# Post-norm attention and ternary FFN on one core: two raw quarters of the second FFN matrix wait in the first norm's columns and in x rows, their sums move behind the first matrix's rounds, and signs take the place of clips

## The reference

```python
x = _layernorm(x + _L0_attn_ref(x, Wq, Wk, Wv, betas, Wo))
x = _layernorm(x + _L0_ffn_ref(x, W1, b1, W2, b2))

def _quantize(W):
    gamma = jnp.mean(jnp.abs(W))
    return jnp.clip(jnp.round(W / (gamma + EPS)), -1.0, 1.0)
# in _L0_ffn_ref: d = 512, d_ff = 2048
Wq1, Wq2 = _quantize(W1), _quantize(W2)
h = jax.nn.relu(jnp.einsum('bsd,fd->bsf', x, Wq1) + b1)
out = jnp.einsum('bsf,df->bsd', h, Wq2) + b2
```

## Time and profile before

| | us |
| --- | --- |
| median of 3 runs (1894.05 to 1895.91) | 1894.54 |
| the profiled execution, its own time | 1894.47 |
| its span | 1892.5 |
| TensorE busy | 1848.2 |
| VectorE busy | 1450.5 |
| ScalarE busy | 1001.9 |
| mean granted TensorE clock | 0.994 |

### The profile page before, as it was taken

How to read it: one execution, slowest core, us unless ns; L and a number is a source line. 1 busy time by engine, 2 the same in 40 slices (tenths; PEclk the granted TensorE clock), 3 DMA queues, 4 the chain that set the end, 5 groups by cost and what they waited for, 6 DMA issues and landing times.

```text
span 1892.5 us, 44351 instructions
## 1 busy us (share of the span) xinstructions
PE 1848.2 (98%) x16447; PEld 1306.4 (69%) x16447; DVE 1450.5 (77%) x2935; ACT 1001.9 (53%) x2422; POOL 765.2 (40%) x775
## 2 busy tenths in 40 slices
PE   5789999999999999999999999999999999999998
PEld 3666677776667776667776677776677776677765
DVE  7868777778777778777777777778777778777774
ACT  5765555555555555555555555555555555555541
POOL 1214334444334444334444334444334444344442
PEclk9899999999999999999999999999999999999999
DMA  8422333422333323323322333323333323233110
GB/s 272 125 44 33 62 58 62 68 48 52 63 59 60 68 44 55 64 55 64 68 47 51 64 59 60 68 48 52 60 62 60 68 47 52 59 59 63 36 24 23
DMA packets 556420, 117.47 MB, mean 62 GB/s; under 512 B 529824, under 2 KB 533808, under 8 KB 555696
## 3 DMA queue, kind: packets, MB, share of 16 engines
q1 hardware_dynamic: 556208, 114.64, 30.9%
HBM read 50.54 MB, written 16.80 MB: 36 GB/s over the span
## 4 chain that ended last, share of the span: by engine, by line
PE 93%; DVE 4%; ACT 1%; SPq 1%; issue 1%; DMA 0%; another core or an unknown queue 0%; POOLq 0%; DVEq 0%; POOL 0%; ACTq 0%
PE bank L433 12%; PE bank L434 12%; PE bank L449 11%; PE bank L450 11%; PE bank L282 6%; PE bank L283 6%; PE bank L284 6%; PE bank L370 3%; PE bank L415 3%; PE bank L414 3%; PE bank L413 3%; PE bank L296 3%; PE bank L349 3%; PE bank L298 3%; PE bank L297 3%; PE bank L401 2%
## 5 line engine op out<-in xcount | busy, mean ns | idle before, releaser
L433 PE MATMUL bank<-yt,w1t 128*128 128x256 f16 x2048 | 453.9, 273 | 0.3 <-DVE yt L811 0.2
L434 PE MATMUL bank<-yt,w1t 128*128 128x256 f16 x2048 | 453.9, 273 | 0.0
L1154 ACT ACTIVATE prob<-bank,exp_bias,gscalars 128x128 f32<-128x128 f32 x512 | 227.7, 456 | 360.4 <-DVE exp_bias L728 356.2
L449 PE MATMUL bank<-w2t,arena 128*128 128x512 f16 x1024 | 388.4, 379 | 0.0
L450 PE MATMUL bank<-w2t,arena 128*128 128x512 f16 x1024 | 388.1, 379 | 0.0
L1198 ACT ACTIVATE arena<-bank,b_scaled,wscalars 128x256 f32<-128x256 f32 x512 | 263.0, 570 | 205.3 <-PE bank L434 151.8
L863 DVE CAST arena<-arena 128x512 f16<-128x512 f32 x256 | 154.3, 603 | 92.8 <-ACT arena L1198 92.0
L1323 POOL TENSOR_TENSOR att_mem<-att_mem,gate_in 128x512 f32<-128x512 f32 x60 | 86.6, 1444 | 330.5 <-DVE att_mem L767 320.2
L433 PEld LDWEIGHTS bank<-yt,w1t 128*128 128x128 f16 x2048 | 200.5, 98 | 23.8 <-issue 0.6
L434 PEld LDWEIGHTS bank<-yt,w1t 128*128 128x128 f16 x2048 | 200.3, 98 | 22.7
L1401 POOL TENSOR_TENSOR arena<-arena 128x512 f16<-128x512 f32 x128 | 155.2, 1213 | 86.1 <-DVE arena L863 86.1
(11 more groups left out here) (186 smaller groups left out, 4299.9 us busy)
## 6 DMA issues: line engine op xcount, KB each, us to landing
rows<-in_L_attn_x SPq DMA_DIRECT2D x32, 512.0 KB, 3.8
out_rows<-rows SPq DMA_DIRECT2D x64, 256.0 KB, 2.3
x_blocks<-in_L_attn_x SPq DMA_DIRECT2D x248, 64.0 KB, 3.0
sk<-sk_t SPq DMA_DIRECT2D x480, 32.0 KB, 2.0
att_dot<-att_mem SPq DMA_DIRECT2D x480, 32.0 KB, 2.0
y_blocks<-rows SPq DMA_DIRECT2D x480, 32.0 KB
arena<-in_L_ffn_W SPq DMA_DIRECT2D x6, 1024.0 KB, 5.3
w2t<-in_L_ffn_W SPq DMA_DIRECT2D x2, 1024.0 KB, 13.1
```

The costliest lines, as they stand in the source:

```text
L433: pe.matmul(ps[:, c], w1t[:, k, cols], yt[:, g % 2, :, k], start=k == 0, stop=False)
L434: ins = pe.matmul(ps[:, c], w1t[:, k, cols], yt[:, g % 2, :, KT + k], start=False, stop=k == KT - 1)
L449: pe.matmul(banks[own][:], h_hi[:, f, toks], w2t[:, f, :], start=f == 0, stop=False)
L1154: ins = act.activation(prob[:, t, at], ps[:, c], ACT.Exp, scale=gcol(g, G_EXP), bias=exp_bias[:, t, at:at + 1], accum_out=row_sum[:, t, h: ...
```

## The change

**Places.** (2,1) now waits in `yt`, the columns of the first norm (both of its halves), (2,3) in rows 1 and 2 of the x buffer; both get semaphores of their own and are loaded early, with no wait for a free arena slot. (2,2) still takes the arena slot of (1,2). Only one copy for a sum remains, that of (2,2); it is loaded behind (1,3) into w1t and is summed by ScalarE where (2,1) was.

**Sums.** VectorE sums (2,1) and (2,3) in their places, behind `round_w(3)`; its two earlier sums are gone. The loads of a turn on SyncE are reordered, and x rows 1 and 2 are loaded at the end of turn g = 1, row 1 behind a wait for all 32 turns.

**Way out.** `put_w` takes Sign(x - ROUND), which is -1, 0 or 1 already. The eight `clip_w` and both waits for them go; `ffn_up` and `ffn_down` wait for `wput` alone.

The diff, without the lists of semaphores:

```diff
@@ -162,7 +162,7 @@
         MOVED = 16 * 16
-        SUM_ORDER = [(1, 1), (1, 3), (1, 0), (1, 2), (2, 0), (2, 1)]
+        SUM_ORDER = [(1, 1), (1, 3), (1, 0), (1, 2), (2, 0), (2, 2)]
         EDGES = (0, NG - 1)
@@ -203,17 +203,21 @@
         def ffn_raw(m, i):
             if m == 1 and i < 2:
                 return w2t[:, 8 * i:8 * i + 8].rearrange("p f n -> p (f n)").bitcast(F32)
+            if (m, i) == (2, 1):
+                return yt[:].rearrange("p g t k n -> p (g t k n)").bitcast(F32)
+            if (m, i) == (2, 3):
+                return rows[:, 1:3].rearrange("p g t d -> p (g t d)")
             return arena[:, (i + 2) % 4, :]
         def ffn_raw_loaded(m, i):
-            if m == 1 and i < 2:
-                return s_raw[4 + i], 16
+            if m == 1 and i < 2 or m == 2 and i % 2:
+                return s_raw[4 + i if m == 1 else 5 + (i + 1) // 2], 16
             slot = (i + 2) % 4
-            return s_raw[slot], {(1, 2): 32, (1, 3): 32, (2, 0): 32, (2, 1): 32, (2, 2): 48, (2, 3): 48}[m, i]
-
-        def for_sum(i):
-            return w1t[:, :, (i - 2) * F // 2:(i - 1) * F // 2].bitcast(F32)
+            return s_raw[slot], {(1, 2): 32, (1, 3): 32, (2, 0): 32, (2, 2): 48}[m, i]
+
+        def for_sum():
+            return w1t[:, :, 0:F // 2].bitcast(F32)
         def w_bank(n):
@@ -424,7 +428,6 @@
                 if n >= 2:
                     pe.wait_ge(sem["relu"], n - 1)
                 else:
-                    pe.wait_ge(sem["clipped"], 4)
                     pe.wait_ge(sem["wput"], NBLOCKS - 3 + n)
                 pe.wait_ge(sem["yt"], by_t(g, 1))
                 for c in range(2):
@@ -442,7 +445,7 @@
                 if piece == 0 and g:
                     pe.wait_ge(sem["res1"], by_t(g - 1, t))
                 elif piece == 0:
-                    pe.wait_ge(sem["clipped"], 8)
+                    pe.wait_ge(sem["wput"], NBLOCKS)
                 pe.wait_ge(sem["h_dve"], 4 * g + piece + 1)
                 pe.wait_ge(sem["h_pool"], 4 * g + piece + 1)
                 for f in range(piece * FT // PIECES, (piece + 1) * FT // PIECES):
@@ -895,9 +898,9 @@
                 dve.scalar_tensor_tensor(out=w_lo[n][:, :, cols], in0=raw[n][:, :, cols], scalar=w(SCALE_W[n]),
                                          in1=w_hi[n][:, :, cols], op0=ALU.mult, op1=ALU.subtract).then_inc(sem["wsplit"], 1)
-            def w_sum(i):
-                dve.wait_ge(s_raw[4 + i], 16)
-                dve.tensor_reduce(w(SUM_PART[2] + i), for_sum(i), AX_XY, ALU.add,
+            def w_sum(m, i):
+                dve.wait_ge(*ffn_raw_loaded(m, i))
+                dve.tensor_reduce(w(SUM_PART[m] + i), ffn_raw(m, i), AX_X, ALU.add,
                                   apply_absolute_value=True).then_inc(sem["wsum_dve"], 1)
             def threshold(m):
@@ -916,12 +919,6 @@
                 dve.wait_ge(*ffn_raw_loaded(m, i))
                 raw_w = ffn_raw(m, i)
                 dve.tensor_scalar(raw_w, raw_w, w(INV_STEP[m]), ROUND, ALU.mult, ALU.add).then_inc(sem["rounded"], 1)
-
-            def clip_w(n):
-                m, i = 1 + n // 4, n % 4
-                dve.wait_ge(sem["wput"], 4 * n + 4)
-                part = w1t[:, :, i * 512:(i + 1) * 512] if m == 1 else w2t[:, :, i * P:(i + 1) * P]
-                dve.tensor_scalar(part, part, 2.0, -1.0, ALU.min, ALU.add).then_inc(sem["clipped"], 1)
             def ffn_scale():
                 dve.wait_ge(sem["bias_turn"], 1)
@@ -986,8 +983,6 @@
                 h_split(g - 2, 5)
                 turn_att(g - 1, 0)
                 qk_split(g, "k", 1)
-                if g == 1:
-                    clip_w(4)
                 if g == 0:
                     w_max("o")
                 turn_att(g - 1, 1)
@@ -999,10 +994,6 @@
                     w_split("v", 0)
                     w_chain("o")
                 qk_split(g, "q", 1)
-                if g == 2:
-                    clip_w(5)
-                    clip_w(6)
-                    clip_w(7)
                 if g == 0:
                     w_split("v", 1)
                 residual(g - 1, 0, 0)
@@ -1020,12 +1011,9 @@
                 turn_x(g + 1, 0)
                 turn_x(g + 1, 1)
                 if g == 0:
-                    w_sum(2)
                     ffn_scale()
                 turn_sk(g)
                 v_split(g, 0)
-                if g == 0:
-                    w_sum(3)
                 invert_sums(g, 0)
                 if g == 0:
                     threshold(1)
@@ -1048,6 +1036,8 @@
                 turn_y(g - 1, 1)
                 if g == 0:
                     round_w(3)
+                    w_sum(2, 1)
+                    w_sum(2, 3)
                 p_split(g, 1, 0)
                 all_max(g + 1)
                 x_scale(g + 1, 0)
@@ -1065,19 +1055,12 @@
                     round_w(4)
                 att_scale(g, 0)
                 read_scale(g, 1)
-                if g == 0:
-                    clip_w(0)
                 xt_lo(g + 1, 0)
                 att_scale(g, 1)
-                if g == 0:
-                    clip_w(1)
                 xt_lo(g + 1, 1)
                 normalise(g - 2, 0, 1)
                 residual(g - 2, 1, 1)
                 h_split(g - 1, 0)
-                if g == 0:
-                    clip_w(2)
-                    clip_w(3)
                 mem_add(g, 0)
                 if g == 0:
                     round_w(5)
@@ -1206,7 +1189,11 @@
             def w_sum(m, i):
                 dst, src = unread, ffn_raw(m, i)
-                act.wait_ge(*ffn_raw_loaded(m, i))
+                if (m, i) == (2, 2):
+                    dst, src = unread.rearrange("p (k f) -> p k f", k=KT), for_sum()
+                    act.wait_ge(s_raw[8], 16)
+                else:
+                    act.wait_ge(*ffn_raw_loaded(m, i))
                 if SUM_ORDER.index((m, i)):
                     act.wait_ge(sem["wsum"], SUM_ORDER.index((m, i)))
                 act.activation(dst, src, ACT.Abs, accum_out=w(SUM_PART[m] + i)).then_inc(sem["wsum"], 1)
@@ -1217,10 +1204,10 @@
                 ps = banks[w_bank(n)][:].rearrange("p (j c) -> p j c", j=4)
                 dst = w1t[:, :, f0:f0 + P] if m == 1 else w2t[:, b * 4:b * 4 + 4, i * P:(i + 1) * P]
                 if n == 0:
-                    act.wait_ge(sem["wsum_dve"], 2)
+                    act.wait_ge(sem["wsum"], 6)
                     act.wait_ge(sem["ones"], 1)
                 act.wait_ge(sem["wturn"], n + 1)
-                act.activation(dst, ps, ACT.Relu, bias=unround[:]).then_inc(sem["wput"], 1)
+                act.activation(dst, ps, ACT.Sign, bias=unround[:]).then_inc(sem["wput"], 1)
             def gates():
                 act.wait_ge(sem["bload"], 16)
@@ -1274,7 +1261,7 @@
                 exponentials(g, 1, 1)
                 p_split(g, 0, 1)
                 if g == 0:
-                    w_sum(2, 1)
+                    w_sum(2, 2)
                     for n in range(0, 4):
                         put_w(n)
                 p_split(g, 1, 0)
@@ -1406,7 +1393,7 @@
                                channel_multiplier=1).then_inc(sem["ident"], 1)
             pool.memset(minus_half[:], -0.5).then_inc(sem["half"], 1)
             pool.memset(ones_all[:], 1.0)
-            pool.memset(unround[:], 1.0 - ROUND)
+            pool.memset(unround[:], -ROUND)
             pool.memset(v1[:, :, :, DV:DV1], 1.0).then_inc(sem["ones"], 1)
             for live in range(LIVE):
                 fill_memory(0, live)
@@ -1447,6 +1434,8 @@
                 if g >= NX:
                     for t in range(TG):
                         sp.wait_ge(s_out[g % NX][t], 16 * (g // NX))
+                if g == 1:
+                    sp.wait_ge(sem["wturn"], NBLOCKS)
                 if g == NX - 1:
                     sp.wait_ge(sem["wsum"], 6)
                 sp.dma_start(rows[:, g % NX], src).then_inc(s_x[g % NX], 16)
@@ -1467,20 +1456,17 @@
             def load_w(n):
                 sp.dma_start(raw[n], dram_w[n].rearrange("(k p) n -> p k n", p=P)).then_inc(s_raw[W_AT[n]], 16)
-            def load_for_sum(i):
-                src = W2.rearrange("(i p) (k f) -> i p k f", p=P, k=KT)[i]
-                sp.dma_start(for_sum(i), src).then_inc(s_raw[4 + i], 16)
+            def load_for_sum():
+                src = W2.rearrange("(i p) (k f) -> i p k f", p=P, k=KT)[2]
+                sp.dma_start(for_sum(), src).then_inc(s_raw[8], 16)
             def load_ffn_w(m, i):
-                before = {(1, 2): "k", (1, 3): "q", (2, 0): "v", (2, 1): "o"}.get((m, i))
-                if before and before != "o":
+                before = {(1, 2): "k", (1, 3): "q", (2, 0): "v"}.get((m, i))
+                if before:
                     sp.wait_ge(sem["wsplit"], 2 * W_ORDER.index(before) + 2)
-                elif before:
-                    sp.wait_ge(sem["wsplit_pool"], 2)
-                if m == 2 and i >= 2:
-                    last = 4 * i + 3
```

(40 more changed lines are left out.)

## The result

The changed kernel's median is 1898.51 us (1896.79 to 1901.63), that of the kernel before 1894.74 us (1894.05 to 1895.91), 18 runs each: a ratio of 1.0019, 95% interval 1.0013 to 1.0026. That is 3.8 us (2.5 to 4.9) more, where 0.9 us more were forecast. It lies inside the stated 1892.6 to 1899.2 us, but above the forecast's own range, which ended at 1898.0 us. A second comparison, with 11 other runs of the changed kernel and 33 of the one before, gave 1898.22 against 1895.96 us, 2.3 us more, with a ratio of 1.0005 (0.9997 to 1.0014). So the kernel is slower by some 2 to 4 us by the medians; the second interval alone would also allow no loss. The profiled execution is the fastest of its 18: 1896.79 us, its span 1895.0.

A forecast was written before the change was run, and what follows sets the result against it. TensorE was taken to bound the kernel, with only its early waits able to change the time. The terms +0.1 + 1.9 - 0.4 - 0.7 = +0.9 us on 1894.5 gave 1895.4 us; own range 1893.1 to 1898.0, stated range 1892.6 to 1899.2 us.

The forecast's parts named there:

- What bounds the kernel: TensorE, nearly always busy from 125 us on; only its waits in the two stages ahead can change the time.
- Leg 1: SyncE's queue up to the second tile's exponentials: later x_blocks and (2,0) give back what two lifted VectorE sums free, +0.1 us.
- Leg 2: VectorE's two sums behind the first matrix's rounds: TensorE waits at its second sum across partitions, +1.9 us.
- Leg 3: Clips gone ahead of the second pair's key and query projections: TensorE's waits there vanish, -0.37 and -0.71 us.
- the other five clips: Clips outside the two projection waits, three of them past 125 us: removing them costs nothing and brings nothing.
- (b): TensorE falls to half clock around the new gap at 70 us: 3 to 5 us more, 1898.4 to 1900.4 us; chance 0.13.
- (a): SyncE's queue is not late, (2,0) comes by 48.7 us: -1.7 us there, 1893.6 us in all; chance 0.22.
- the sign that I had named as wrong: TensorE's granted clock under 1.00 between 68 and 90 us would show the forecast wrong.
- (c): VectorE bounds the early stages, so eight clips of 0.6 us count: -4.8 us, 1889.7 us; chance 0.08.
- (d): Sign isn't in ScalarE's loaded table, so extra table loads cost +5 to +6.5 us: 1900.5 us; chance 0.02.
- Covered edits: Later x rows, (2,2)'s load, later key moves and Sign for Relu are hidden behind other work and cost nothing.

The follow-up runs named there:

- after_again: The changed kernel, unaltered, timed and profiled again in a second comparison: 1898.22 us, ratio 1.0005 to the kernel before.
- e4: The changed kernel with TensorE's second sum across partitions moved behind the first attend and turns 8 and 9: 1896.82 us, ratio 1.0006 to the kernel before.
- e10: The changed kernel with VectorE's sum of (2,3) cut to 128 of 2048 columns, making the output off: 1896.67 us, ratio 0.9997 to the kernel before.
- e1: The kernel before with only the way out by Sign and without the eight clips: 1895.34 us, ratio 0.9993.
- e3: The kernel before with only x rows 1 and 2 loaded later, at the end of turn g = 1: ratio 0.9999.
- e2: The changed kernel with Relu and the eight clips back, so only places, sums and queue differ from before: 1899.41 us, ratio 1.0017.
- e9: The changed kernel with the load of (2,0) ahead of (2,1) in SyncE's queue: 1898.70 us, ratio 1.0011 to the kernel before.
- before_again: The kernel before, unaltered, timed and profiled again: ratio 0.9998.

## Why the prediction was right in its sign and short in its size

- **What bounds the kernel: right.** All the edits acted before u, and what they did there is what they did to the time: the ratio of every row of the table agrees within 1.5 us with its sum from s to u, taken against the 81.2 us of the two profiles of before. Behind u no edit shows an effect that stands out of the spread.
- **Leg 1: the mechanism right, the term mis-sized.** Forecast +0.1 us, measured 21.2 against 19.4 us: **+1.8 us**. Counted from s, to leave out the chance start, x_blocks came as forecast (5.8 us behind s for 5.7). Two steps failed. (2,0) was put at 50.5 us, which is 11.1 behind s, and came at 12.7 and 12.4, so the exponentials ended 1.3 to 1.5 us late. The rate was as forecast at first and then not: once x_blocks was there the DMA moved 392 GB/s for 4.8 us (398 for 4.7 in after_again), and then 103 (108) GB/s for the 2 us up to the landing of (2,0). What held this last part is not shown. And "so that comes to 53.6 us", VectorE's V remainder (14.2 behind s), came at 16.8 and 16.2: I had moved its chain rigidly by the wait less the lifted sum. From the start of the maximum to the end of the V remainder VectorE took 11.0 and 10.4 us, where the rigid shift leaves 8.5. Shifted by 2.7 us against its neighbours, its first gate operation met GpSimd's split and took 1.89 us for 0.67, ending when that ended (47.19 and 47.17 us); the transposes began 0.4 us later behind the score bias than before; and `ffn_scale` took 3.3 us for 2.5 with TensorE at half clock, 2.7 in after_again with TensorE at full clock. So the scores waited for VectorE, which I had thought 0.7 us ahead, and would have come 1.3 to 1.5 us late for ScalarE alone.
- **Leg 2: right.** Forecast +1.9, measured +1.2 to +1.8 us (12.75 against 10.9 to 11.5, by how long the kernel before stayed at half clock), and the same wait is taken away by e4 and e10.
- **Leg 3: right.** Forecast -1.1, measured -1.2 us; its mark for the key projection, 82.4 us, had left out the 0.4 us that the sum takes off. xt had more room than forecast: before, it began inside GpSimd's `att_mem` and took 1.77 us; without the clip it begins ahead of that and takes 0.74 us. This gained no time, since TensorE came later still, but the kernel before had paid for more than the clip. One of "the other five clips" did bring something: q to u is 0.25 us shorter in every kernel without clips. By its place it is the one at the start of the second pair, the only one in that stretch: before, it stands at 91.00 us, and TensorE falls behind e1 by 0.2 us some 5.4 us behind q, at 92.3 us. No run takes it out alone.
- **The sum.** +1.8 +1.5 -1.2 = +2.1 us at q, forecast +0.9, and +1.9 us at u. The first comparison gave 2.5 to 4.9 us, the second -0.6 to +2.7. What lies between the 1.9 of the traces and the 3.8 of the first is not settled: start and late stretch vary by 1.6 and 5 us between the profiles here, whatever the kernel.
- **Luck.** The 3.8 us of the first comparison are more than the upper end of the three legs' own range, 3.5. They fall inside the stated range because that took in half of rival (b), which did not happen.
- **The rivals.** (a) is out: the queue was late. (b) is out as priced: in the changed kernel's profile the granted clock was 1.00 from 68 us on, over the 1.34 us gap too. In after_again it was still 0.50 to 0.62 up to 70 us and 1.00 behind, the sign that I had named as wrong, but that was the end of the old half-clock stretch and no new fall; e to t was the same 12.75 us. Half clock did add some 0.6 us to leg 1 in one profile. (c) and (d) fell with e1.
- **Covered edits: right**, as far as tried; the late rows by e3; the key moves, issued from 61.43 us on instead of 55.34, by the absence of any wait at the memory update. (2,2)'s round has no wait in the profile.

## What to carry to other kernels

A load added to a shared queue costs what stands behind it, on every engine that consumes it: find the consumers that have slack and put it ahead of those alone; here the same bytes, later in the queue, made 3.5 us in the trace and 3 to 4 us in the time. Where two engines wait side by side, one edit shows little and both show all, so test them together before giving a cause up. An instruction that waits in the order of the bounding engine should stand as late as its own consumer allows: moving one small matmul behind an attend and two turns took 1.5 to 1.7 us off the traces. And a chain doesn't shift rigidly: its short steps meet other neighbours, and have to be priced there.

## What the runs showed that I had not expected

- A VectorE operation on 128 x 4 elements took 1.89 us in the changed kernel, ending 0.02 us behind a two-input fp32 operation of GpSimd that had started 0.26 us ahead of it. This is not one chance meeting. In six of the profiles (after, after_again, e2, e4, e10, and e9 one gate operation later) a gate operation of this size began inside that split and ended 0.02 to 0.03 us behind it, whenever it had begun; in the others it took 0.18 to 0.77 us. So the 0.67 us of the profile before were no fixed cost either: before_again has 0.18. It also fits e9: there x_blocks came 0.7 us earlier behind s than in after_again, and the V remainder no earlier (16.2 us behind s in both), with the same split between. No run moved the split itself, so this is read from the times alone.
- The xt step, 128 x 512 with two inputs from SBUF, behaves alike beside GpSimd's `att_mem`: begun well inside it, it ended 0.54 to 0.56 us behind it (before, before_again, e3, e1, e2: 0.94 to 1.77 us long), begun ahead of it, it took 0.74 us.
- SyncE's issues of the y_blocks moves, 0.61 us each in the middle, have some of 3.8 to 5.8 us in every profile, at about the same places of the program. In the changed kernel the 16 of one turn took 15.21 us:

```profile
614.19 15.21 SPq L1507 DMA_DIRECT2D y_blocks<-rows  x16
```

In such a turn TensorE is sometimes short of work; in the longest late stretch, e9's, TensorE waited for 5.5 us in all behind 125 us, in the first profile of before for 1.1 us. The largest of e9's waits (us in total, times, longest):

```profile
PE bank L353 <- ACT prob L1137: 3.5, 3, 1.9
...
PE bank L374 <- DVE pt_lo L740: 1.4, 3, 0.6
```

That the slow issues make these waits, and these the spread of the last column, is an inference; no experiment was made on it.
